# Second cross attention of a perceiver kernel: the copy of each score tile's lower half goes from the vector to the scalar engine, and the second batch's transfers go from the layer norm's block to the attention's own

## What is computed

```python
def _L1_xattn_ref(query, key):
    a = jnp.einsum('bqd,bkd->bqk', query, key)
    e = jax.nn.softmax(a, axis=-1)
    c = jnp.einsum('bqk,bkd->bqd', e, key)
    return c
...
x = x + _L1_xattn_ref(_layernorm(x, axis=-1), ctx_4096)
```

## Time and profile before

| | before |
|---|---|
| median of 3 runs | 2850.13 us (2843.49 to 2854.75) |
| profiled execution, its time | 2852.12 us |
| profiled execution, its span | 2850.3 us |
| PE, DVE, ACT, POOL busy | 92%, 68%, 53%, 52% of the span |
| layer norm block of the second cross attention | 2393.0 to 2405 us of the span |
| its attention block | 2405.7 to 2584.4 us |

### The profile page before, as it was taken

One profiled execution on the slowest core, in us unless ns is written; L12 is line 12 of the kernel. 1 busy time (PEld: TensorE's weight loads), 2 busy tenths in 40 slices (PEclk: granted clock), 3 DMA queues, 4 the chain that ended last, 5 costly groups with the idle time before them and its releaser, 6 DMA issues. The chain is left out here.

```text
span 2850.3 us, 43003 instructions
## 1 busy us (share of the span) xinstructions
PE 2609.3 (92%) x17032; PEld 2379.1 (83%) x17032; DVE 1933.5 (68%) x2204; ACT 1520.6 (53%) x2694; POOL 1494.5 (52%) x1009
## 2 busy tenths in 40 slices
PE   7999999999999999999999999989856667997788
PEld 6899999999999999999999999987732225775677
DVE  2266776777677667767776776674559997786773
ACT  3455665566566556655665565554344442663552
POOL 2344754655555564574584385430019961793752
PEclk9999999999999999999999999999968988998879
DMA  5410110111110011011011110015140003441100
GB/s 201 134 46 23 61 51 26 61 46 31 46 60 24 25 52 61 24 53 57 27 54 46 38 46 31 23 36 212 57 150 10 0 15 118 131 125 45 50 1 15
DMA packets 90700, 164.81 MB, mean 58 GB/s; under 512 B 8146, under 2 KB 57554, under 8 KB 87946
## 3 DMA queue, kind: packets, MB, share of 16 engines
q1 hardware_dynamic: 82186, 153.75, 16.1%
q10 hardware_dynamic: 8320, 8.39, 0.9%
HBM read 144.22 MB, written 17.89 MB: 57 GB/s over the span
## 5 line engine op out<-in xcount | busy, mean ns | idle before, releaser
L357 POOL TENSOR_TENSOR xa_pt_lo<-xa_st,xa_pt_hi 128x1024 fp32r<-128x1024 f32 x255 | 510.4, 2036 | 595.3 <-ACT xa_pt_hi L543 595.3
L54 PE MATMUL xa_kv_ps<-ctx_wv_hi,ctx_hi 128*128 128x256 f32 (+1 forms) x1664 | 468.1, 281 | 3.1 <-DVE xa_v_lo L634 3.1
L56 PE MATMUL xa_kv_ps<-ctx_wv_hi,ctx_lo 128*128 128x256 f32 (+1 forms) x1664 | 470.1, 283 | 0.0
L55 PE MATMUL xa_kv_ps<-ctx_wv_lo,ctx_hi 128*128 128x256 f32 (+1 forms) x1664 | 465.8, 280 | 0.0
L54 PE MATMUL xa_kv_ps<-ctx_hi,ctx_wk_hi 128*128 128x402 f32 (+1 forms) x1024 | 357.0, 349 | 2.2 <-DVEq L711 2.2
L56 PE MATMUL xa_kv_ps<-ctx_hi,ctx_wk_lo 128*128 128x402 f32 (+1 forms) x1024 | 353.7, 345 | 0.0
L55 PE MATMUL xa_kv_ps<-ctx_lo,ctx_wk_hi 128*128 128x402 f32 (+1 forms) x1024 | 353.3, 345 | 0.0
L634 DVE TENSOR_TENSOR xa_v_lo<-xa_kv_ps,xa_v_hi 128x512 fp32r<-128x512 f32 (+1 forms) x224 | 146.3, 653 | 266.7 <-ACT xa_v_hi L516 265.7
L54 PEld LDWEIGHTS xa_kv_ps<-ctx_wv_hi,ctx_hi 128*128 128x128 f32 (+1 forms) x1664 | 306.9, 184 | 3.3 <-DVE xa_v_lo L634 3.3
L55 PEld LDWEIGHTS xa_kv_ps<-ctx_wv_lo,ctx_hi 128*128 128x128 f32 (+1 forms) x1664 | 309.0, 186 | 0.0
L56 PEld LDWEIGHTS xa_kv_ps<-ctx_wv_hi,ctx_lo 128*128 128x128 f32 (+1 forms) x1664 | 307.2, 185 | 0.0
(11 more groups left out here) (407 smaller groups left out, 7031.9 us busy)
## 6 DMA issues: line engine op xcount, KB each, us to landing
ca_nat<-in_ctx SPq DMA_DIRECT2D x48, 512.0 KB, 3.9
ctx_raw<-in_ctx_t SPq DMA_DIRECT2D x24, 804.0 KB, 6.6
ctx_wk_raw<-in_xa_wk SPq DMA_DIRECT2D x64, 256.0 KB, 2.8
ctx_wv_raw<-in_xa_wv SPq DMA_DIRECT2D x32, 512.0 KB, 4.4
q_raw<-in_xa_wq SPq DMA_DIRECT2D x8, 1024.0 KB, 4.9
q_scratch<-q_q_sb ACTq DMA_DIRECT2D x8, 1024.0 KB, 4.4
xa_q_raw<-q_scratch SPq DMA_DIRECT2D x64, 128.0 KB, 2.6
o_scratch<-xa_o_sb SPq DMA_DIRECT2D x64, 128.0 KB, 1.7
```

Of the source, the lines that this page charges most:

```text
L54: nc.tensor.matmul(out, left[0], right[0], start=first, stop=False)
L55: nc.tensor.matmul(out, left[0], right[1], start=False, stop=False)
L56: return nc.tensor.matmul(out, left[1], right[0], start=False, stop=last)
L357: nc.gpsimd.tensor_tensor(by_chunk(pt_lo, p), scored(j, p).rearrange("p g q c -> p g c q"), by_chunk(pt_hi, p).bitcast(F32), ALU.subtract) ...
```

## The change

`load_first` issues batch 0 alone. The attention block's SP program issues batch 1 first, then batches 2 to 7 as before. The copy of partitions 64 to 127 of each score tile is taken off DVE and is now a scalar-engine `activation` Copy (`lower_half`), put in ACT's order of `SCORES` where DVE's `joined` stands in DVE's. From the third tile of the program on, it waits for `s_free` of the tile two before, which was the last to read its half of `part_sb`. The last group's `natural` keeps its place. DVE's `joined` is the wait for `part_set` and the addition.

```diff
         def load_first(sp):
-            for b in range(2):
-                for g in range(NG):
-                    load(sp, b, g)
+            for g in range(NG):
+                load(sp, 0, g)
...
         @block.sync
         def _(sp):
+            for g in range(NG):
+                load(sp, 1, g)
             for b in range(2, B):
...
+            def lower_half(b, t):
+                c, w = TILES[t]
+                w = min(w, S - c)
+                n = b * NT + t
+                act.wait_ge(s_full, n + 1)
+                if n >= 2:
+                    act.wait_ge(s_free, n - 1)
+                nc.scalar.activation(part_sb[:, t % 2, 0:w], s_ps[L:2 * L, t % 2, 0:w], ACT.Copy).then_inc(part_set, 1)
+
...
                     for kind, at, part in SCORES:
                         if kind == "t":
                             high(b + 1, at)
-                        if kind == "t" and at == EARLY + 1 and b >= 0:
-                            natural(b, NG - 1)
+                            if at == EARLY + 1 and b >= 0:
+                                natural(b, NG - 1)
+                        elif part == len(PARTS) - 1:
+                            lower_half(b + 1, at)
...
                 c, w = TILES[t]
                 w = min(w, S - c)
-                dve.wait_ge(s_full, b * NT + t + 1)
-                nc.vector.tensor_copy(part_sb[:, t % 2, 0:w], s_ps[L:2 * L, t % 2, 0:w]).then_inc(part_set, 1)
                 dve.wait_ge(part_set, b * NT + t + 1)
                 nc.vector.tensor_tensor(prob[:, c:c + w], s_ps[0:L, t % 2, 0:w], part_sb[:, t % 2, 0:w],
                                         ALU.add).then_inc(s_free, 1)
```

## The result

| | before | after |
|---|---|---|
| median of 10 runs | 2850.64 us | 2838.11 us |
| range of the runs | 2843.49 to 2854.75 us | 2834.25 to 2846.45 us |
| profiled execution | 2852.12 us | 2837.09 us |
| its span, mean granted clock | 2850.3 us, 0.955 | 2835.3 us, 0.957 |

The ratio is 0.9957, 95% interval 0.9946 to 0.9968: 12.5 us, or 0.43%, less. The forecast was 2840, within 0.5% of before.

The account below looks back on a forecast made before the run. PE was taken to bound the attention's batches, waiting for DVE's `low` twice a batch and for SP's issues at the border; 3.25 + 5.3 + 0.8 + 0.6 = 9.95 us less gave 2840 us, range 2833 to 2848.

Parts of the forecast that it names:

- The border: Between layer norm and attention blocks: with seven issues fewer on SP, PE starts 3.25 us earlier.
- Seven issues at no cost: Batch 1's issues in the attention's block: nobody waits for their data, 1.6 us of room at the worst.
- Rival (d): Batch 1's data land late and PE waits; slower, 2851 us with twice the slowest landing; chance 0.04.
- The copy in batches 2 to 7: Copies moved from DVE to ACT: 0.88 us less in each of six batches, 5.3 us in all.
- the two places: Where PE waits for DVE's `low` each batch: before chunk 12 (1.21 us) and at tile 3's start (0.27 us).
- the remaining wait of half a microsecond: Before chunk 12 in batches 2 to 7: 0.6 us of PE's wait stays.
- Its cover: ACT's slack at `high` of chunk 9 before DVE would wait for it: 0.45 us.
- At chunk 12: One copy fewer on DVE before `low` of chunk 10: chunk 12 starts 0.61 us earlier.
- At tile 3: Two copies fewer on DVE before `low` of chunk 12: the 0.27 us before tile 3's first matmul go.
- Batches 0 and 1: Copies moved to ACT in the first two batches: 0.8 us and 0.6 us less.
- Rival (a): First transposes and gap before batch 1: clock rises sooner or never falls; gain 14.7 us, 2835; chance 0.16.
- rival (c): Attention start, batch 1 or last `pv`: lower clock, or half the start; gain 5 to 7 us, 2844; chance 0.09.

Follow-up runs that it names:

- e1: Kernel before with batch 1's seven issues moved into the attention's block, copies left on DVE; ratio to before 0.9993.
- e2: Changed kernel with all fourteen issues back in the layer norm's block, copies kept on ACT; ratio to before 0.9978.
- e5: Changed kernel with thirteen of the fourteen issues in the layer norm's block, batch 1's last group alone in the attention's; ratio to before 0.9974.
- e7: Changed kernel with ACT copying each lower half twice, first into a spare tile that nobody reads; ratio to before 0.9971.
- e10: Changed kernel with thirteen matmuls that nobody reads in PE's idle time before batch 1's chunks 3 and 5; median 2835.47 us, ratio to before 0.9950.
- e3: Changed kernel with ACT copying tiles 0 and 1 only, DVE copying tiles 2 and 3 as before; ratio to before 0.9965.
- e9: Changed kernel with DVE's residual moved behind the scores' last `low` and ACT's `natural` behind `high` of chunk 12; median 2835.01 us, ratio to before 0.9950.
- e12: The changed kernel run once more, unedited, on the same chip as e9 to e11; median 2835.24 us, ratio to before 0.9950.
- e6: Changed kernel with batch 1's seven transfers issued by POOL in the layer norm's block, SP issuing only batch 0's there; ratio to before 1.0003.
- e11: e9 and e10 together, plus eight matmuls that nobody reads ahead of the last product; median 2836.09 us, ratio to before 0.9956.
- e4: Changed kernel with ACT copying tiles 2 and 3 only, DVE copying tiles 0 and 1 as before; ratio to before 0.9988.
- e8: Changed kernel with DVE's residual of the previous batch moved behind the last `low` of the scores; median 2838.25 us, ratio to before 0.9963.

## Why the prediction came out right, point by point

**The border.** The term was 3.25 us and is 3.25 in the ledger, e1 alone gives 3.26, and before, e2 and e5 put it on SP's issues: PE follows the last one by 0.98, 0.98 and 0.88 us, wherever it ends. Seven issues at no cost also held. The first group of batch 1 landed 4.9 us after its issue at 2401.03, where the bound was 12.8, and PE wanted it at 2415.44; PE has no wait for a transfer in the trace. Rival (d) fell. The remark from the Trainium skill on double-buffering ("Trainium Kernel Development and Optimization", Best Practices) made the prediction look for a wait here. The trace shows none: batch 1's transfers still overlap with batch 0's compute, and only their issues moved.

**The copy in batches 2 to 7.** The sign, the two places and the remaining wait of half a microsecond were right, and so was ACT's copy (506 ns estimated, 504 measured). Its cover was not: 0.16 us and not 0.45. The size per batch was short: 0.88 us predicted, 1.09 measured. Both terms were too small.
- At chunk 12 the copy counted 0.61 us, from its own start to the addition's. From the start of `low` of chunk 7 to that of chunk 9 it is 2498.32 - 2495.91 = 2.41 us before and 2489.74 - 2488.06 = 1.68 after: **0.73 us**. Before, the copy began 0.03 us behind the end of `low`, and the addition 0.03 behind the copy's; now the addition begins 0.07 us ahead of that `low`'s end. The additions and the `low`s around them start some 0.07 us ahead of the end of the instruction before; around the copy that overlap was missing twice. The addition reads the copy and waits for it, but the copy needs nothing of `low`. What the two have in common with ACT's rows in e7 is that the copy reads from partition 64 on and its neighbours from partition 0 on. On ACT that goes with 0.12 us per change; that it is the same on DVE is likely and not shown alone. The row to read was the start-to-start of what stood on either side.
- On ACT the same was missed the other way. `natural`, the copy and `high` of chunk 9 were taken to follow each other with the overlaps of the earlier trace rows, 0.52 + 0.51 = 1.03 us from the start of `natural` to that of `high`. It is 2488.98 - 2487.80 = 1.18 us. These 0.15 us, and the 0.12 by which DVE came sooner than thought, took the cover from 0.45 to the 0.16 that was left; a slightly longer copy would have started to eat the gain.
- At tile 3 the count was 0.27 us, up to its first matmul. From chunk 12's start to `pv`'s first matmul it was 3.61 us and is 2494.39 - 2491.16 = 3.23: **0.38**. The timeline of PE before shows where the other 0.1 us was: the matmul behind the late one starts 0.29 us after it, those that follow 0.18.

```profile
2501.80 0.45 PE L1881 MATMUL ca_s_ps<-ca_t_hi,n_xt 128*128 128x396 f32 x1
2502.09 0.53 PE L1886 MATMUL ca_s_ps<-ca_t_lo,n_xt 128*64 128x396 f32 x2
2502.45 0.34 PE L1881 MATMUL ca_s_ps<-ca_t_hi,n_xt 128*128 128x396 f32 x1
...
2503.35 0.40 PE L1907 MATMUL ca_c_ps<-ca_n_hi,ca_pt 128*128 128x512 f32 x1
```

So a matmul that started late cost PE 0.11 us once more behind it; why isn't shown. Six times 0.21 is 1.27 us of the 2.24 by which the stretch's sum was short.

**Batches 0 and 1.** Batch 0 gave the 0.49 us worked out for chunk 12. Batch 1 gave 0.20 to its chunk 12 instead of 0.62: its wait there went from 0.79 only to 0.62.

**The clock.** It was kept out of the sum as rivals (a) and (c). A part of each came, at other places than they named. Windows around the last product, before and then after:

```profile
2571.00:2584.40 13.40, 9.33 (x42) 6.08 (x40) 10.92 (x13) 3.66 (x7) 0.64 (x1) 0.87 0.00 0
```

```profile
2558.00:2572.00 14.00, 8.84 (x45) 5.50 (x43) 11.60 (x16) 4.65 (x9) 1.34 (x2) 0.98 0.00 0
```

Before, the clock was at 1.2 GHz from 2576.3 to 2579.7 us, within the last product; after, windows of 2 us each show 1.00 up to 2570, and PE is through with the product at 2569.2. That is some 1.3 of the last part's 1.70 us, tile 3 being the rest. The prediction named this place only for a loss, in rival (c), so these 1.3 us are luck. Rival (a) had looked for a gain at the start and in the gap before batch 1, and neither came: batch 1 ran at a mean of 0.83 in both. The Trainium skill's rule on idle gaps ("TensorE: Matmul & The Clock Gate", Why this matters for your kernels) agrees in its direction with e10, where work in the gap kept the full clock. What decides the last product isn't told by the length of the gap ahead of it. PE's wait there is 2.4 to 2.5 us in most kernels, and the clock held in four of them (after, e3, e9, e12) and fell in the others; in e6 it fell after a wait of only 1.5 us, in e7 after 2.8, and in e11, which fills the wait, it held. From chunk 12 of batch 7 to the last residual it took 20.9 to 21.0 us where the clock held, and 22.1 to 22.6 where it fell for 3.4 us (before, e1, e4, e5, e7, e8, e10; 21.3 in e6, with its shorter wait); in e2 it was low for 6.8 us, and the part took 23.35.

**The median.** 12.5 us gained against 9.95: from 9.92, 1.27 more for the two terms in six batches, 0.1 for tile 3 in the last part and some 1.3 for the clock at the end, less 0.4 in batch 1, give the stretch's 12.19. So 1.4 us of the excess come from two terms that were read too small, the rest from a clock that was not forecast. That the medians' difference lies close to the stretch's is as good as ten runs can say.

## What to carry to other kernels

An engine that only issues transfers can hold the barrier of a block as long as an engine that computes: leave in a block what must be issued there, and look at the gap between the last compute and the first of the next block, not at whether the transfers land in time. Of work that is to leave a full engine, only what stands in its order ahead of something that the bounding engine waits for is worth moving (tiles 0 and 1 here, all of the gain; tiles 2 and 3, none), and its price is read from the start of what stood before it to the start of what stood behind, on the engine that it leaves and on the one that it goes to. The next engine is close: after 1.1 us of 20.6 ACT and the residual were in the way, and after another 0.5 probably POOL.

## What was not expected of the hardware

- SP's issue of the same 512 KB took 0.38 us at first, 0.56 at the eighth and 1.17 at the thirteenth, and the fourteenth, though only 130 KB, took 1.68; issued in the next block, the first five of batch 1's seven took 2.43 us together, 0.49 each.
- Whether two instructions in a row overlap on ACT went with the partition from which they read: by 0.10 us where both began at the same one, and not at all where one read from 0 on and the other from 64 on (e7). In the changed kernel `natural`, 0.62 us long, holds ACT for 0.65 us up to the copy's start, where it held it for 0.52 before.
- POOL issued seven in 5.10 us, but the border came only after its last landing, 12.50 us behind the last compute (e6).
- Whether the clock falls in the last product differs between kernels whose code there is the same, and repeated in the one kernel profiled twice (after and e12). Thirteen matmuls added some 140 us earlier (e10) went with a fall. What links the two is open.
